# One reaction tile in PSUM, the identity after the transposition, and a new order of work, in a four-stage conditional kernel

## What is computed

```python
# stage 1: attention pooling, mask by kind (prefix, postfix, all but itself)
attn_in = tanh(x @ W1 + b1); scores = attn_in @ v
p = softmax(where(mask[kind], scores, -1e30)); x = x + (p @ x) / count
# stage 2: adapter by language (10 of them), with a layer norm
y = x + relu(x @ W1[lang] + b1[lang]) @ W2[lang] + b2[lang]
x = x + layernorm(y) * gamma[lang] + beta[lang]
# stage 3: reaction and diffusion, edges reflected
x = x + zX * (left - 2*x + right) + zY * (up - 2*x + down) + zR * x * (1 - x)
# stage 4: matrix by category (64 of them)
x = x + x @ W[cat] + b[cat]
```

## Time and profile before

| | |
|---|---|
| median of 3 runs | 1095.55 us (1087.53 to 1095.93) |
| the profiled execution | 1097.21 us |
| its span in the trace | 1095.4 us |
| mean granted TensorE clock | 0.998 |
| busy: TensorE, VectorE, ScalarE, GpSimd | 1055.9, 956.5, 504.8, 710.9 us |
| DMA moved | 268.92 MB, 246 GB/s |

### The profile page before, as it was taken

The page is one execution under the profiler, slowest core; times in us unless marked ns, Lnnn a source line. Parts: engine busy times, 40 slices in busy tenths (PEclk is TensorE's granted clock), DMA queues, the critical chain, the costliest instruction groups (busy, mean ns, idle before and its releaser), DMA issues.

```text
span 1095.4 us, 23744 instructions
## 1 busy us (share of the span) xinstructions
PE 1055.9 (96%) x4912; PEld 656.8 (60%) x4912; DVE 956.5 (87%) x1962; ACT 504.8 (46%) x1422; POOL 710.9 (65%) x665
## 2 busy tenths in 40 slices
PE   6799999999999999999999999999999999999996
PEld 3565666656655656666665566665666565566562
DVE  5799989989989899999888888989898898999994
ACT  3444444444444444445444444444444444444441
POOL 3467667666666676667657666767665766667765
PEclk9999999999999999999999999999999999999999
DMA  8688798678779977876786868887879788897873
GB/s 346 199 260 236 247 293 244 203 250 254 245 230 288 298 239 237 246 229 203 228 266 193 265 198 255 269 266 235 269 241 262 228 268 237 288 276 226 244 241 115
DMA packets 134732, 268.92 MB, mean 246 GB/s; under 512 B 29139, under 2 KB 29157, under 8 KB 127173
## 3 DMA queue, kind: packets, MB, share of 16 engines
q1 hardware_dynamic: 97476, 199.83, 58.7%
q10 hardware_dynamic: 37120, 67.58, 20.4%
HBM read 243.21 MB, written 33.55 MB: 253 GB/s over the span
## 4 chain that ended last, share of the span: by engine, by line
PE 54%; issue 21%; POOL 17%; DVE 6%; DVEq 1%; ACTq 0%; ACT 0%; DMA 0%; POOLq 0%; SPq 0%
PE ps_out L429 23%; POOL b_wide L892 6%; PE ps_adapt L411 6%; PE bank_hidden L383 6%; PE ps_attn L361 6%; PE ps_pool L402 6%; POOL neighbours L873 4%; POOL react L879 3%; PE ps_x3T L419 3%; POOL rstd L865 2%; DVE x L764 2%; PE bank_scores L372 2%; PE bank_hidden L395 1%; DVE res L739 1%; POOL above L885 1%
## 5 line engine op out<-in xcount | busy, mean ns | idle before, releaser
L429 PE MATMUL ps_out<-w3s,x3T 128*128 x1024 | 490.1, 601 | 2.3 <-ACT x3T L496 2.3
L885 POOL TENSOR_TENSOR above<-above,below 128x512 f32<-128x512 f32 x128 | 166.7, 1303 | 226.7 <-DMA above<-x 223.7
L429 PEld LDWEIGHTS ps_out<-w3s,x3T 128*128 128x128 f32 x1024 | 185.1, 191 | 190.6 <-issue 188.7
L764 DVE SCALAR_TENSOR_TENSOR x<-above,wide_rows,react 128x512 f32<-128x512 f32 x128 | 189.5, 1481 | 13.9 <-POOL above L885 12.5
L879 POOL TENSOR_TENSOR react<-react,x 128x512 f32<-128x512 f32 x128 | 175.5, 1371 | 2.4 <-ACT react L539 2.4
L892 POOL TENSOR_TENSOR b_wide<-b_wide,x 128x512 f32<-128x512 f32 x128 | 173.1, 1352 | 1.7 <-DMA b_wide<-in_b 1.7
L865 POOL TENSOR_TENSOR rstd<-var_eps,minus_half 128x1 f32<-128x1 f32 x128 | 70.2, 549 | 132.0 <-DVE var_eps L731 131.9
L517 ACT ACTIVATE square_junk<-ps_adapt,neg_mean 128x512 f32<-128x512 f32 x128 | 88.1, 688 | 139.1 <-DVE neg_mean L692 139.1
L411 PE MATMUL ps_adapt<-w_all,hid 128*128 x256 | 133.0, 601 | 12.6 <-DVE x L746 12.2
L383 PEld LDWEIGHTS bank_hidden<-w_all,xts 128*128 128x128 f32 x1024 | 124.4, 192 | 28.4 <-issue 26.4
L383 PE MATMUL bank_hidden<-w_all,xts 128*128 x1024 | 137.2, 277 | 0.0
(11 more groups left out here) (111 smaller groups left out, 1281.3 us busy)
## 6 DMA issues: line engine op xcount, KB each, us to landing
w3s<-in_w SPq DMA_DIRECT2D x128, 1024.0 KB
xts<-in_xT ACTq DMA_DIRECT2D x128, 256.0 KB, 4.7
xs<-in_x ACTq DMA_DIRECT2D x128, 256.0 KB, 5.0
b_wide<-in_b SPq DMA_DIRECT2D x128, 256.0 KB, 4.2
out_x<-res SPq DMA_DIRECT2D x128, 256.0 KB, 3.4
below<-x SPq DMA_DIRECT2D x128, 252.0 KB
above<-x SPq DMA_DIRECT2D x128, 252.0 KB
below<-x SPq DMA_DIRECT2D x256, 2.0 KB
```

The source lines that it names most:

```text
L429: mm = pe.matmul(ps_out[j.ring(2)][:, :], x3T[:, j.ring(2), k * P:(k + 1) * P], w3s[:, bass.ds(wslot * (K * D) + k * D, D)], start=(k == 0 ...
L764: nc.vector.scalar_tensor_tensor(x3[:, q, :], above[:, q, :], zy_t[:, bass.ds(i.n, 1)], react[:, q, :], ALU.mult, ALU.add).then_inc(x3_rea ...
L885: nc.gpsimd.tensor_tensor(above[:, q, :], above[:, q, :], below[:, q, :], ALU.add).then_inc(rows_ready, 1)
```

## The change

- The reaction term is one PSUM bank (ps_react) instead of two SBUF buffers. ScalarE writes `nzr * x2 + c0` there. The product with x2 moves from GpSimd to VectorE. The bank is single, so ScalarE's reaction waits for add_rows of the item before, not of two before.
- ScalarE makes `mix = probs * scale` (scale_rows), TensorE transposes it, and VectorE adds the identity on the way from ps_mixT to mixT (add_identity). mix_rows on VectorE and the copy on ScalarE are gone.
- ps_out is one bank instead of two: category of an item waits for the result of the item before.
- The order of the steps is new on all five engines, and some items come a slot later. adapter_project waits for relu of the item before instead of two before; shift_rows waits also for x3 of two before. SP's list is now shift_rows(s), load_params of one value and load_b3(s-1), load_params of one value and store(s-3), load_params of three values and load_w3(s).

```diff
-        react = sb("react", [P, 2, D])
+        ps_react = pb("ps_react")
-        ps_out = [pb("ps_out0"), pb("ps_out1")]
+        ps_out = pb("ps_out")
...
             def shift_rows(i):
                 q = i.ring(2)
                 sp.wait_ge(x2_ready, i.upto())
+                if i.is_at_least(2):
+                    sp.wait_ge(x3_ready, i.upto(2))
                 for to, at, rows, source in ((below, 0, P - 2, 1), (above, 2, P - 2, 1),
                                              (below, P - 2, 1, P - 1), (below, P - 1, 1, P - 2),
                                              (above, 0, 1, 1), (above, 1, 1, 0)):
@@ -282,16 +284,18 @@
 
             def slot(s):
                 if s.inside(B):
+                    shift_rows(s)
+                if (s - 1).inside(B):
+                    cat_m1, = load_params(sp, CAT, 1, s - 1)
+                    load_b3(s - 1, cat_m1)
+                if (s - 3).inside(B):
+                    item_m3, = load_params(sp, ITEM, 1, s - 3)
+                    store(s - 3, item_m3)
+                if s.inside(B):
                     cat, fresh, wslot = load_params(sp, CAT, 3, s)
-                    shift_rows(s)
                     load_w3(s, cat, fresh, wslot)
-                if (s - 2).inside(B):
-                    item_m2, = load_params(sp, ITEM, 1, s - 2)
-                    store(s - 2, item_m2)
-                if s.inside(B):
-                    load_b3(s, cat)
-
-            run_slots(slot, 0, B + 1)
+
+            run_slots(slot, 0, B + 4)
...
-                if s.is_at_least(2):
-                    pe.wait_ge(relu_ready, s.upto(2))
+                if s.is_at_least(1):
+                    pe.wait_ge(relu_ready, s.upto(1))
...
-                    if j.is_at_least(2):
-                        pe.wait_ge(res_ready, j.upto(2))
+                    if j.is_at_least(1):
+                        pe.wait_ge(res_ready, j.upto(1))
...
+                if s.inside(B):
+                    attn_project(s)
+                if (s - 5).inside(B):
+                    wslot, = load_params(pe, WSLOT, 1, s - 5)
+                    category(s - 5, wslot, range(2, K))
+                if (s - 1).inside(B):
+                    adapter_hidden(s - 1)
                 if s.inside(B):
                     kind, = load_params(pe, KIND, 1, s)
...
+                    attn_scores(s, kind)
+                if (s - 1).inside(B):
+                    pool(s - 1)
+                if (s - 4).inside(B):
+                    x3_transpose(s - 4)
                 if s.inside(B):
...
+                    lang, = load_params(pe, LANG, 1, s)
+                    adapter_project(s, lang)
+                if (s - 1).inside(B):
+                    lang_m1, = load_params(pe, LANG, 1, s - 1)
+                    adapter_up(s - 1, lang_m1)
+                if (s - 4).inside(B):
+                    wslot_next, = load_params(pe, WSLOT, 1, s - 4)
+                    category(s - 4, wslot_next, range(0, 2))
                 if s.inside(B):
                     mix_transpose(s)
...
-            def move_mixT(b):
-                act.wait_ge(mixT_mm, b.upto())
+            def scale_rows(b):
+                p = b.ring(2)
+                act.wait_ge(scale_ready, b.upto())
+                act.wait_ge(probs_ready, b.upto())
                 if b.is_at_least(2):
-                    act.wait_ge(pool_mm, b.upto(2))
-                nc.scalar.activation(mixT[:, b.ring(2), :], ps_mixT, ACT.Copy).then_inc(mixT_ready, 1)
+                    act.wait_ge(mixT_mm, b.upto(2))
+                nc.scalar.activation(mix[:, p, :], probs[:, p, :], ACT.Copy, scale=scale[:, p:p + 1]
+                                     ).then_inc(mix_ready, 1)
...
-                if h.is_at_least(2):
-                    act.wait_ge(x3_ready, h.upto(2))
-                nc.scalar.activation(react[:, h.ring(2), :], x2[:, h.ring(2), :], ACT.Identity,
+                if h.is_at_least(1):
+                    act.wait_ge(x3_ready, h.upto(1))
+                nc.scalar.activation(ps_react[:, :], x2[:, h.ring(2), :], ACT.Identity,
                                      bias=c0_t[:, bass.ds(h.n, 1)], scale=nzr_t[:, bass.ds(h.n, 1)]
                                      ).then_inc(react_ready, 1)
...
-            def mix_rows(b):
-                p = b.ring(2)
-                dve.wait_ge(scale_ready, b.upto())
+            def add_identity(b):
+                dve.wait_ge(mixT_mm, b.upto())
                 if b.is_at_least(2):
-                    dve.wait_ge(mixT_mm, b.upto(2))
-                nc.vector.scalar_tensor_tensor(mix[:, p, :], probs[:, p, :], scale[:, p:p + 1], ident[:, :],
-                                               ALU.mult, ALU.add).then_inc(mix_ready, 1)
+                    dve.wait_ge(pool_mm, b.upto(2))
+                nc.vector.tensor_tensor(mixT[:, b.ring(2), :], ps_mixT, ident[:, :], ALU.add).then_inc(mixT_ready, 1)
...
+            def react_times_x2(i):
+                q = i.ring(2)
+                dve.wait_ge(react_ready, i.upto())
+                nc.vector.tensor_tensor(ps_react[:, :], ps_react[:, :], x2[:, q, :], ALU.mult).then_inc(react_x2_ready, 1)
+
             def add_columns(i):
                 q = i.ring(2)
                 dve.wait_ge(react_x2_ready, i.upto())
                 dve.wait_ge(neighbours_ready, i.upto())
                 dve.wait_ge(edges_ready, i.upto())
-                nc.vector.scalar_tensor_tensor(react[:, q, :], neighbours[:, q, :], zx_t[:, bass.ds(i.n, 1)],
-                                               react[:, q, :], ALU.mult, ALU.add).then_inc(columns_ready, 1)
...
+                if (s - 2).inside(B):
+                    normalize(s - 2)
+                if (s - 5).inside(B):
+                    result(s - 5)
+                if (s - 1).inside(B):
+                    add_b2(s - 1, lang)
                 if s.inside(B):
                     denominator(s)
-                if h.inside(B):
-                    add_adapted(h)
+                    row_scale(s)
+                if (s - 1).inside(B):
+                    add_adapted(s - 1)
+                if (s - 3).inside(B):
+                    react_times_x2(s - 3)
+                if (s - 1).inside(B):
+                    mean(s - 1)
+                    add_beta(s - 1, lang)
+                if (s - 3).inside(B):
+                    add_columns(s - 3)
                 if s.inside(B):
-                    row_scale(s)
-                if h.inside(B):
-                    mean(h)
-                if s.inside(B):
-                    mix_rows(s)
+                    add_identity(s)
+                if (s - 1).inside(B):
+                    add_epsilon(s - 1)
                 if (s - 3).inside(B):
                     add_rows(s - 3)
-                if (s - 4).inside(B):
-                    result(s - 4)
-                if h.inside(B):
-                    add_epsilon(h)
-                    center(h, lang)
-                if (s - 2).inside(B):
-                    add_columns(s - 2)
-                if h.inside(B):
-                    normalize(h)
-
-            run_slots(slot, 0, B + 3)
+                if (s - 1).inside(B):
+                    center(s - 1, lang)
...
-            def react_times_x2(i):
-                q = i.ring(2)
-                pool.wait_ge(react_ready, i.upto())
```

More of the change, by code:

```diff
@@ L391, in adapter_hidden @@
             def adapter_hidden(f):
-                if (f + 1).inside(B):
-                    pe.wait_ge(xw_ready, (f + 1).upto())
+                pe.wait_ge(xw_ready, f.upto())
                 pe.wait_ge(mixT_ready, f.upto())
@@ L425, in category @@
                     pe.wait_ge(w3_in[j.ring(2)], j.dma())
-                    if j.is_at_least(2):
-                        pe.wait_ge(res_ready, j.upto(2))
+                    if j.is_at_least(1):
+                        pe.wait_ge(res_ready, j.upto(1))
                 for k in ks:
-                    mm = pe.matmul(ps_out[j.ring(2)][:, :], x3T[:, j.ring(2), k * P:(k + 1) * P],
+                    mm = pe.matmul(ps_out[:, :], x3T[:, j.ring(2), k * P:(k + 1) * P],
                                    w3s[:, bass.ds(wslot * (K * D) + k * D, D)], start=(k == 0), stop=(k == K - 1))
@@ L574, in slot @@
             def slot(s):
+                if s.is_first:
+                    item, = load_params(act, ITEM, 1, s)
+                    load_xT(s, item)
+                    load_x(s, item)
+                    for i in range(4, L):
+                        move_b2(i)
+                elif s.inside(B):
+                    item, = load_params(act, ITEM, 1, s)
+                    load_xT(s, item)
+                if (s - 3).inside(B):
+                    variance(s - 3)
+                if (s - 1).inside(B):
+                    attn_tanh(s - 1)
@@ L575, in slot @@
+                if (s - 1).inside(B) and not (s - 1).is_first:
+                    item_m1, = load_params(act, ITEM, 1, s - 1)
+                    load_x(s - 1, item_m1)
```

(46 more changed lines are left out.)

55 lines of the change are left out of this document (14 added, 41 removed).

## The result

The changed kernel takes **1144.88 us** (median of 4 runs, 1141.66 to 1154.15), the kernel before 1095.74 beside it: ratio 1.047, 95% interval 1.038 to 1.056. The forecast was 1106 with 1070 to 1130: the direction was right, the size was not, and the time lies outside the range.

A forecast was written before the change was run, and what follows sets the result against it. SP's DMA-issue queue was to set the pace at 8.30 us a slot against 8.216: +0.084 x 127 = +10.7 us on a 1095.4 span, 1106.1; with surroundings 1107.9, less 1.7: 1106 us. Eight in 10 between 1070 and 1130.

The forecast's parts named there:

- the 24 us of stalls: TensorE's waits above its floor in the kernel before, about 24 us, forecast not to be won.
- TensorE's floor: Matmuls without a gap from one mix transposition to the next: 8.04 us a slot, unchanged by the new order.
- The single banks, relu, the x3T copy and scale_rows: One bank each for category product and react, earlier relu wait, x3T copy, ScalarE's scaling: each costed at zero.
- The weight directly ahead of the shifts: SP's weight issue just before the next shifts: taken as zero, between -0.21 and +0.34 us a slot.
- the sum for SP: SP's work per slot: 7.86 us plus 0.44 for the new load, 8.30, above TensorE's 8.04.
- The price of the new load: SP's added one-value load of CAT for load_b3: 0.44 us a slot, between 0.28 and 0.55.
- The base of 7.86: SP's work in the kernel before: 7.86 us of every 8.22 us slot, waits taken off.
- Start and end stay: Before the first and after the last weight issue, time unchanged: same chain to x2(0), same final steps.
- TensorE idle before the x3 transposition: Sign of a right forecast: TensorE waits there for x3 from late shifts, 0.26 us a slot.
- The third rival: The weight in front of the shifts holds them: SP at 8.40 to 8.60, 1119 to 1144 us; chance 0.15.
- The first rival: TensorE keeps the pace, the new load being absorbed in SP's queue: 1066 to 1080 us; chance 0.20.
- point of decision: SP work per slot from which SP, not TensorE, sets the pace: given as 8.07 us.

The follow-up runs named there:

- a_merge: The changed kernel with four row-shift DMAs in place of six, rows 0 and 127 together: 1077.06 us, ratio 0.983.
- b_own_shift: The kernel before, with load_b3 taking its category from an extra one-value load directly behind the six shifts: 1129.11 us, ratio 1.033.
- a_keep: The changed kernel without the extra load; load_b3 uses the register filled for the weight a slot earlier: 1091.83 us, ratio 0.998.
- b_merge: The kernel before with four row-shift DMAs in place of six: 1090.57 us, ratio 0.996.
- a_w3place: The changed kernel with the three-value load and the weight directly behind the shifts, then b3 with its own load and the store: 1122.57 us, ratio 1.024.
- b_own_b3: The kernel before, with an extra one-value load for b3 behind the store, directly ahead of load_b3: 1097.99 us, ratio 1.002.

## Why the prediction was right and wrong

Right was which engine sets the pace: SP, whose waits go away, so that none of the 24 us of stalls is won. TensorE's floor stayed (8.05). VectorE came to 873.6 / 128 = 6.83 us a slot (6.90 forecast) and add_rows to 0.74. The single banks, relu, the x3T copy and scale_rows cost nothing: with SP relieved in a_merge, TensorE runs at 8.04 a slot with all of them in place. The weight directly ahead of the shifts was costed at zero, "the same loss at another place", and this is what the shifts show (0.66 us after a fresh weight, 0.65 before).

The span was forecast at 1106.1 and came to 1142.4, 36.3 us more. The step that failed is the sum for SP, 7.86 + 0.44 = 8.30 us a slot, against 8.54 measured:
- **The price of the new load, 0.44 us, was mis-sized.** It was SP's own row of one value, but that stood behind a weight's issue. Where the change puts it, behind the one-row shifts, the load takes 0.71; its gap is 0.76 longer, and the next load 0.20 shorter, net 0.56. That lies just above my upper bound of 0.55, which came from ACT. 0.12 a slot, 15 us. Measured directly, SP's work grows by 0.46 a slot in b_own_shift and falls by 0.49 in a_keep, for the same load. (The Trainium skill, DMA: Bandwidth & Descriptors, section Latency and other measured facts, has some 600 ns as the floor of a load: the rows do not agree, since a load at another place takes 0.28.)
- **The base of 7.86 was too low.** I took all of SP's waits off the 127 slots, but 8.3 us of them lie behind the last weight issue. The base is 7.93: 0.07 a slot, 8 us. The gap ahead of the store says the same: it is on the mean 0.18 above its median (0.87 and 0.69), as 22.9 us over 127 slots are.
- The loads and steps that moved take 0.04 a slot more in their new places: 5 us. SP's waits, which I had at zero, are 0.02: 3 us. Together 7.93 + 0.56 + 0.04 = 8.53, against 8.54 measured; that the parts close so well is partly luck, since medians stand beside means here.
- **"Start and end stay" failed for the start**: 6.6 us later, 3.3 of it given back at the end. I followed the queues in the middle of the run only. ScalarE's new list puts the second transposed x behind the b2 copies.

**Where the stalls come from was wrong as well**, though the time doesn't hang on it. I put TensorE's stalls on x3 and the late shifts, before and after. In the kernel before, it waits more for normalize, ahead of adapter_up, than for x3 (12.2 us in 17 slots against 4.0 in 4), and relieving SP wins 5 us and not 24 (b_merge). In the changed kernel it waits, as I read the trace, for fresh category matrices. The sign "TensorE idle before the x3 transposition" did not come.

The third rival almost has the time that came (1119 to 1144, with SP at 8.40 to 8.60), but not the cause: a_w3place separates the two, and the weight in front of the shifts does not hold them longer than a weight further ahead. The first rival, that the load is absorbed, is what b_own_b3 shows for another place of the same load. (Its point of decision, 8.04 + 3 / 127, is 8.06 and not 8.07; nothing hangs on it.)

What stays open: why a load behind the one-row shifts takes longer than one behind the weight or b3. The trace shows the times, and nothing that SP waits for in them. Nor are they fixed: in a_keep the load of three values, which is the same as in the changed kernel, has a gap of 1.63 instead of 1.38 once the load two issues ahead is gone.

## What to carry to other kernels

Count a queue that only issues DMAs as an engine: add up its issues and register loads in a slot, set them against the pace, and price a new load by rows behind the same kind of instruction as it will have ahead of it. Take off only the waits that lie in the stretch from which the pace is taken. A value that is in a register already costs nothing to keep for a slot, and rows at both ends of a tile can go in one DMA; here that gave 53 and 68 us, while the change itself was worth 13.5 once SP was out of the way. Follow a new order through the first slots as well, and see in the trace that an instruction added for a measurement is there.

## What the runs showed of the hardware that I had not expected

- A load of one value on SP takes 0.28 us behind a b3 issue or a skipped weight and 0.71 behind the one-row shifts. Of two loads one after another with one short issue between, the second is 0.2 to 0.3 us shorter than it is without the first.
- A fresh 1 MB weight makes the shifts 0.65 us later or longer, whether it was issued directly ahead or with b3 and the store in between (0.5 in a_w3place, in the shifts' issue alone).
- Issuing a DMA of two far rows takes as long as one of one row, 0.6 us.
- The same add_rows, with the same operands in SBUF and the same work on GpSimd, takes 1.75 us at the median in the kernel before and 0.74 in b_merge. I read this as the work of what runs beside it at that moment.
- TensorE's clock stood at 0.51 in the stretch after 3.33 us of waiting at the start, and the time is paid twice: the wait, and 2.07 us in place of 1.06 for the next eight matmuls.
